# A three-layer cross network with a ReLU tower: layer 2 fed before layer 1 is normalized, one norm matmul for three layers, other orders of the first loads and of the top layers

## The chip, the cores and the metric

The kernel runs on one core of one Trainium2 chip. The metric is the device time of one launch in microseconds (us); lower is better. Three timed runs of the kernel before gave 1300.02, 1300.39 and 1301.56 us, median 1300.39.

## The reference

Everything is fp32. For each of 512 samples, 39 table rows of 16 numbers are gathered (`e`, 512 x 39 x 16). Three cross layers follow, each with 128 units; `ws[k]` and `bs[k]` are their weights and biases:

```python
prev = x                                   # b, 39, 16
for k in range(3):
    z = jnp.einsum('bmd,bhd->bdmh', x, prev).reshape(b, D, m * h)
    t = jnp.einsum('bdc,co->bdo', z, ws[k]) + bs[k]
    t = jnp.transpose(t, (0, 2, 1))
    norm = jnp.sqrt(jnp.sum(t * t, axis=(-2, -1), keepdims=True))
    t = t / norm
    logit.append(t)
    prev = t
z = jnp.sum(jnp.concatenate(logit, axis=1), axis=-1)          # b, 384
h = jnp.concatenate([z, dense_ctx], axis=1)                   # b, 400
h = jnp.maximum(h @ W_top1 + b_top1, 0.0)                     # 512
h = jnp.maximum(h @ W_top2 + b_top2, 0.0)                     # 256
y = h @ W_top3
```

The norm is one number for each sample, over all 128 units and 16 positions. Below the layers are called layer 0, 1 and 2.

## The kernel before, in words

The batch is cut into 16 tiles of 32 samples. In a tile, the free axis of every operand has 512 columns (32 samples times 16 positions, `N`), and the partitions hold fields or units.

**Gather.** GpSimd computes row numbers and issues ten indirect DMAs a tile into `gathered` (L154), waits for them, writes the rows to DRAM (`xt`, L162 and L164), waits for that and goes on to the next tile. It runs far ahead: every tile has its own place in `xt`.

**Loads.** SyncE's queue (SP) brings the tile's rows back. `load_layer0` (L184 to L190) issues eight DMAs: three copies of the 39 fields into `x3` and the shifted fields into `xr`. `load_fields` (L199) issues thirteen DMAs of 768 KB into `xb`, in which each field is repeated over all 128 partitions; chunk c holds three fields. For every tile but the first, chunk c is loaded when layer 2 of the tile before has used it. The weights of layers 1 and 2 (`w1`, `w2`, 2.5 MB each) are issued at the very start from ScalarE's queue (L224, L225).

**Layer 0.** VectorE multiplies `x3` by each of the seven steps of `xr` into `z0` (`products0`, L295) and TensorE accumulates seven matmuls into `acc[0]` (L392). It is symmetric, so seven steps of three shifts do.

**Layers 1 and 2.** VectorE multiplies three fields at a time, 128 x 1536 numbers, by the layer before (`t_ps[0]` or `t_ps[1]`, in PSUM) into one of four slots of `z` (`products`, L308; thirteen chunks a layer), and TensorE runs three matmuls on each chunk (`layer`, L405). An fp32 matmul shows as two instructions in the trace, so a layer is 78 of them.

**Normalizing.** After each layer, ScalarE squares the accumulator and adds the bias (L243, L245), VectorE sums both over positions (`sum_squares`, L316 and L318), TensorE adds over partitions with a matmul with ones on 32 columns (`add_partitions`, L414), ScalarE takes the root (L250), and VectorE refines the inverse (`normalize`, L328 to L335), writes the normalized layer to `t_ps[k]` (L339, layers 0 and 1) and the sums to `feat` (L344). All three layers have a chain of their own.

**Order.** Each engine's program is written out by hand. In tile i, TensorE runs layer 1 of i, layer 0 of i+1, layer 2 of i. VectorE runs the products of layer 1 (with the sums and the normalizing of layer 2 of tile i-1 put between chunks), `products0(i + 1)`, then the whole normalizing of layer 1 of tile i, and then the products of layer 2 (with the normalizing of layer 0 of tile i+1 between chunks).

**Top.** After the last tile, the weights of the tower lie in the space of `xb` (loaded after the last product), and TensorE runs 16 matmuls for the first dense layer (L453, L454; three accumulators, the fourth output block waits for one), 8 for the second (L459) and 2 for the output (L464).

Of the kernel before, what the change touches and what calls it, by code (L numbers as in the profile page):

```python
# [35 lines left out]


CH = 3
CHUNKS = FIELDS // CH
ZSLOTS = 4  # L40

TOP1, TOP2 = 512, 256
DENSE = 16


def build(nc, ids_in, base_in, table, xt, dense_t, w0a, w0b, w1, w2, b0, b1, b2,
          wt1, bt1, wt2, bt2, wt3, out):
    ctx = ExitStack()
    with ctx:
# [15 lines left out]
        z0 = sb("z0", [WIDE, STEPS0, N])  # L65
# [6 lines left out]
        ones = sb("ones", [P, P])  # L72
        traw = sb("traw", [P, LAYERS, N])
# [8 lines left out]
        feat = sb("feat", [P, LAYERS, BATCH])  # L82
        dense_sb = sb("dense_sb", [DENSE, BATCH])
        bt1_sb = sb("bt1_sb", [P, TOP1 // P])
        bt2_sb = sb("bt2_sb", [P, TOP2 // P])
        wt3_sb = sb("wt3_sb", [P, TOP2 // P])

        top = xb[:, :, :].rearrange("p m n -> p (m n)")
        wt1_sb = top[:, 0:LAYERS * TOP1].rearrange("p (k o) -> p k o", k=LAYERS)
        wt1d_sb = top[0:DENSE, LAYERS * TOP1:4 * TOP1]  # L90
        wt2_sb = top[:, 4 * TOP1:4 * TOP1 + 4 * TOP2].rearrange("p (k o) -> p k o", k=4)
# [6 lines left out]
        nrm = [pb(f"nrm{k}") for k in range(LAYERS)]  # L98
# [6 lines left out]
        w_loaded = [None, sem("w1_loaded"), sem("w2_loaded")]  # L105
        small_loaded = sem("small_loaded")
        w0_ready = sem("w0_ready")
        ones_ready = sem("ones_ready")
        x0_loaded = sem("x0_loaded")
# [4 lines left out]
        acc0_ready = sem("acc0_ready")  # L114
        raw_ready = [sem(f"raw_ready{k}") for k in range(LAYERS)]
        ssum_ready = [sem(f"ssum_ready{k}") for k in range(LAYERS)]
        nrm_ready = [sem(f"nrm_ready{k}") for k in range(LAYERS)]
        root_ready = [sem(f"root_ready{k}") for k in range(LAYERS)]
        step_done = sem("step_done")
        rnorm_ready = [sem(f"rnorm_ready{k}") for k in range(LAYERS)]  # L120
        t_ready = [sem("t0_ready"), sem("t1_ready")]
        feat_ready = [sem(f"feat_ready{k}") for k in range(LAYERS)]
        top_loaded = sem("top_loaded")
# [3 lines left out]


        ZSTEPS = 2 * CHUNKS

        def slot_free(i, s):

            if s >= ZSLOTS:
                return ZSTEPS * i + s - ZSLOTS + 1
            last = max(r for r in range(ZSTEPS) if r % ZSLOTS == s)
            return None if isinstance(i, int) and i == 0 else ZSTEPS * (i - 1) + last + 1
# [4 lines left out]
        def _(pool):  # L141
            nc.gpsimd.memset(ones[:, :], 1.0).then_inc(ones_ready, 1)
            pool.wait_ge(ids_loaded, 32)

            def gather(i):


# [9 lines left out]
                pool.wait_ge(rows_gathered, 16 * GROUPS * (i + 1))  # L157

                for first, rows in ((0, FIELDS), (FIELDS, SHIFTS - 1)):
                    full, rest = divmod(rows, GROUP)  # L160
                    blk = xt[bass.ds(i, 1), first:first + rows, :].rearrange("a m n -> (a m) n")
                    pool.dma_start(blk[0:full * GROUP, :].rearrange("(g f) (b d) -> (f b) g d", f=GROUP, d=EMB),  # L162
                                   gathered[:, 0:full, :]).then_inc(xt_written, 16)
                    pool.dma_start(blk[full * GROUP:rows, :].rearrange("f (b d) -> (f b) d", d=EMB),  # L164
                                   gathered[0:rest * TILE_B, full, :]).then_inc(xt_written, 16)

                pool.wait_ge(xt_written, 64 * (i + 1))

            with pool.Fori(0, TILES) as i:
                gather(i)  # L170

        @block.sync
        def _(sp):
# [5 lines left out]
            def load_layer0(i):  # L179

# [11 lines left out]
            def load_fields(i):  # L192
                later = not (isinstance(i, int) and i == 0)
                for c in range(CHUNKS):
                    if later:

                        sp.wait_ge(z_ready, ZSTEPS * (i - 1) + CHUNKS + c + 1)
# [85 lines left out]
        def _(dve):  # L283
# [14 lines left out]
            def products(i, k, c):  # L298

                s = (k - 1) * CHUNKS + c  # L300
                if c == 0:
                    dve.wait_ge(t_ready[k - 1], i + 1)
# [210 lines left out]
```

## Time and profile before

| | |
|---|---|
| median of three timed runs | 1300.39 us |
| span of the profiled execution | 1297.4 us |
| TensorE matmul busy | 1217.8 us, 94% |
| VectorE busy | 904.4 us, 70% |
| ScalarE busy | 78.1 us, 6% |
| GpSimd busy | 205.2 us, 16% |
| DMA | 203.70 MB, mean 157 GB/s |

The profiled execution has its span alone as its time, from the first instruction to the last; the timed runs are 3.0 us longer at the median, which lies around the span. In the rows below, "PE" is TensorE's matmuls, "DVE" VectorE, "ACT" ScalarE, "SPq" the DMA issues of SyncE. A row of the chain says when a piece began, how long it was on the chain and what it was; x78 counts instructions. A row of the windows shows a stretch, the busy time of each engine in it, then the granted TensorE clock as a share of full speed, the mean busy share of the 16 DMA engines, and GB/s.

### The profile page before, as it was taken

How to read it: one execution, taken by the hardware profiler on the slowest of the kernel's cores; microseconds unless marked ns; L12 is line 12 of the kernel's file. 1: busy time of each engine (PE TensorE's matmuls, PEld its weight loads, DVE VectorE, ACT ScalarE, POOL GpSimd, SP SyncE). 2: the span in 40 equal slices, each digit the busy share in tenths (PEclk: the TensorE clock that was granted, in tenths of full speed). 3: DMA queues.
4: the chain of work that ended last, by engine and by line, in shares of the span. 5: the costliest groups of instructions: out<-in, count | busy, mean ns of one | idle time of the engine just before them, and what ended most of it. 6: DMA issues, size and time to landing. Idle time of an engine off the chain costs nothing.

```text
span 1297.4 us, 9951 instructions
## 1 busy us (share of the span) xinstructions
PE 1217.8 (94%) x2868; PEld 538.6 (42%) x2868; DVE 904.4 (70%) x898; ACT 78.1 (6%) x155; POOL 205.2 (16%) x245
## 2 busy tenths in 40 slices
PE   0599999999999999999999999999999999999898
PEld 0244444444444444444444444444444444444343
DVE  0468877777787777778777777887777788777640
ACT  0100000000000000000000000000000000000001
POOL 5554654546440000000000000000000000000000
PEclk9899999999999999999999999999999999999998
DMA  7938356290935528092653809165380917444010
GB/s 221 361 58 314 75 195 194 70 316 12 325 63 202 170 87 285 0 323 49 219 153 107 265 0 332 39 233 138 121 250 9 330 32 254 118 145 170 1 41 0
DMA packets 58974, 203.70 MB, mean 157 GB/s; under 512 B 11131, under 2 KB 14331, under 8 KB 58966
## 3 DMA queue, kind: packets, MB, share of 16 engines
q1 hardware_dynamic: 47478, 195.26, 46.1%
q0 software_dynamic: 7424, 3.19, 1.8%
q10 hardware_dynamic: 4064, 5.15, 1.2%
q8 instruction: 4, 0.07, 0.0%
q14 instruction: 4, 0.03, 0.0%
HBM read 201.67 MB, written 1.90 MB: 157 GB/s over the span
## 4 chain that ended last, share of the span: by engine, by line
PE 91%; DVE 4%; issue 2%; DMA 2%; ACT 1%; POOL 1%; SPq 0%; POOLq 0%; ACTq 0%
PE acc L405 83%; PE acc L392 5%; DVE z L308 2%; PE acc L453 1%; DMA xr<-xt 1%; PE nrm L414 1%; POOL gathered L154 1%; PE t_ps L459 1%; DVE inv L328 1%; DMA gathered<-in_table,rows_of 0%; PE acc L454 0%; ACT root L250 0%; DVE prod L330 0%; DVE rnorm L335 0%; DVE half L332 0%
## 5 line engine op out<-in xcount | busy, mean ns | idle before, releaser
L405 PE MATMUL acc<-z,w_sb 128*128 128x512 f32 x2496 | 1087.4, 596 | 27.4 <-DVE z L308 27.4
L308 DVE TENSOR_TENSOR z<-t_ps,xb 128x1536 f32<-128x1536 f32 x416 | 711.9, 1751 | 186.0 <-PE acc L405 185.6
L405 PEld LDWEIGHTS acc<-z,w_sb 128*128 128x128 f32 x2496 | 472.4, 191 | 617.7 <-issue 545.8
L154 POOL DMA_INDIRECT gathered<-in_table,rows_of x160 | 154.3, 964 | 57.6 <-issue 43.9
L392 PE MATMUL acc<-z,w_sb 117*128 117x512 f32 (+1 forms) x224 | 104.4, 609 | 40.7 <-DVE z L295 40.7
L316 DVE TENSOR_REDUCE ssum<-sq 128x32 f32<-128x512 f32 x48 | 32.6, 679 | 111.6 <-ACT traw L245 111.6
L295 DVE TENSOR_TENSOR z<-x,xr 117x512 f32<-117x512 f32 (+1 forms) x112 | 68.8, 682 | 29.5 <-DMA xr<-xt 29.5
L243 ACT ACTIVATE sq<-acc,bias 128x512 f32<-128x512 f32 x48 | 33.0, 687 | 808.8 <-PE acc L405 771.8
L392 PEld LDWEIGHTS acc<-z,w_sb 117*128 117x128 f32 (+1 forms) x224 | 42.1, 194 | 88.1 <-issue 87.1
L162 POOL DMA_DIRECT2D xt<-gathered x32 | 29.8, 932 | 76.9 <-DMA gathered<-in_table,rows_of 74.4
L245 ACT ACTIVATE traw<-acc,bias 128x512 f32<-128x512 f32 x48 | 32.7, 681 | 0.0
L318 DVE TENSOR_REDUCE dsum<-traw 128x32 f32<-128x512 f32 x48 | 32.4, 675 | 0.0
L414 PEld LDWEIGHTS nrm<-ssum,ones 128*128 128x128 f32 x96 | 18.2, 193 | 31.6 <-issue 21.5
L328 DVE RECIPROCAL inv<-root 128x32 f32<-128x32 f32 x48 | 16.6, 345 | 19.1 <-ACT root L250 18.8
L250 ACT ACTIVATE root<-nrm 128x32 f32<-128x32 f32 x48 | 9.5, 198 | 335.9 <-PE nrm L414 335.8
L339 DVE TENSOR_TENSOR t_ps<-traw,rnorm 128x512 f32<-128x512 f32 x32 | 22.4, 699 | 1.1
L414 PE MATMUL nrm<-ssum,ones 128*128 128x32 f32 x96 | 15.2, 240 | 7.6 <-DVE ssum L316 7.6
L164 POOL DMA_DIRECT2D xt<-gathered x32 | 18.1, 564 | 0.0
L453 PE MATMUL acc<-feat,xb 128*128 128x512 f32 x24 | 14.0, 728 | 1.7 <-DVE feat L344 1.7
L148 POOL TENSOR_TENSOR rows_of<-ids_sb,base_sb 128x10 int32<-128x10 int32 x16 | 3.1, 196 | 48.3 <-DMA xt<-gathered 45.3
L344 DVE TENSOR_TENSOR feat<-dsum,rnorm 128x32 f32 (+1 forms) x48 | 8.9, 186 | 2.3 <-DVE rnorm L335 2.2
L335 DVE SCALAR_TENSOR_TENSOR rnorm<-half,inv 128x32 f32<-128x32 f32 x48 | 9.2, 191 | 1.6
(23 smaller groups left out, 51.1 us busy)
## 6 DMA issues: line engine op xcount, KB each, us to landing
xb<-xt SPq DMA_DIRECT2D x208, 768.0 KB, 6.4
xr<-xt SPq DMA_DIRECT2D x48, 468.0 KB
x<-xt SPq DMA_DIRECT2D x48, 78.0 KB
gathered<-in_table,rows_of POOLq DMA_INDIRECT x160
xr<-xt SPq DMA_DIRECT2D x32, 78.0 KB
xt<-gathered POOLq DMA_DIRECT2D x16, 72.0 KB, 2.9
xb<-in_wt SPq DMA_DIRECT2D x1, 768.0 KB, 4.6
xt<-gathered POOLq DMA_DIRECT2D x32, 6.0 KB, 2.1
```

The costliest lines, as they stand in the source:

```text
L154: nc.gpsimd.indirect_dma_start(gathered[0:n, g, :], None, table[:, :], bass.IndirectOffsetOnAxis(rows_of[0:n, g:g + 1], 0)).then_inc(rows_ ...
L162: pool.dma_start(blk[0:full * GROUP, :].rearrange("(g f) (b d) -> (f b) g d", f=GROUP, d=EMB), gathered[:, 0:full, :]).then_inc(xt_written ...
L243: nc.scalar.activation(sq[:, k, :], acc[k][:, :], ACT.Square, bias=bias[:, k:k + 1]).then_inc(raw_ready[k], 1)
L245: nc.scalar.activation(traw[:, k, :], acc[k][:, :], ACT.Identity, bias=bias[:, k:k + 1]).then_inc(raw_ready[k], 1)
L295: nc.vector.tensor_tensor(z0[0:n, k, :], x3[0:n, :], xr[0:n, k, :], ALU.mult).then_inc(z0_ready, 1)
L308: nc.vector.tensor_tensor(z[:, s % ZSLOTS, :, :], fields_of(k, c), xb[:, c * CH:(c + 1) * CH, :], ALU.mult).then_inc(z_ready, 1)
L316: nc.vector.tensor_reduce(ssum[:, k, :], sq[:, k, :].rearrange("p (b d) -> p b d", d=EMB), axis=AX_X, op=ALU.add).then_inc(ssum_ready[k], 1)
L318: nc.vector.tensor_reduce(dsum[:, k, :], traw[:, k, :].rearrange("p (b d) -> p b d", d=EMB), axis=AX_X, op=ALU.add).then_inc(step_done, 1)
L328: nc.vector.reciprocal(inv[:, k, :], root[:, k, :]).then_inc(step_done, 1)
L392: last = nc.tensor.matmul(acc[0][:, :], w0_sb[0:n, k, :], z0[0:n, k, :], start=(k == 0), stop=(k == STEPS0 - 1))
L405: last = nc.tensor.matmul(acc[k][:, :], w_sb[k][:, m, :], z[:, s % ZSLOTS, r, :], start=(m == 0), stop=(m == FIELDS - 1))
L414: nc.tensor.matmul(nrm[k][:, 0:TILE_B], ones[:, :], ssum[:, k, :], start=True, stop=True).then_inc(nrm_ready[k], 1)
```

## The change

Four things are changed together.

1. **Layer 2 gets layer 1 with its bias but without its norm.** ScalarE writes `acc[1]` plus bias straight to `t_ps[1]`; `products(i, 2, c)` waits for that alone. As layer 2 is linear in layer 1 up to its bias, the accumulator of layer 2 is multiplied by layer 1's inverse norm afterwards, once, by VectorE (`scale2`, in the next tile's layer 1 after chunk 2), into `scaled`, from which ScalarE makes the squares and the biased copy.
2. **One norm event a tile.** The sums of layer 2 of tile i-1, layer 1 of tile i and layer 0 of tile i+1 lie side by side in `ssum`; one matmul of 96 columns (`add_partitions`, after chunk 4 of layer 2), one root and one `normalize` (after chunk 6) serve them all. `feat` is written for three layers at once.
3. **First loads and queues.** GpSimd only gathers; the writes to `xt` and the wait for them stand in SyncE's queue (`write_rows`). `products0` writes its result over `xr`, so that the loads of tile i+1 wait for `acc0_ready` of tile i, and `xr` is loaded in four groups with a semaphore each. For the first tile ScalarE's queue loads `x3`. `w1` is cut into thirteen pieces, issued by SyncE between the pieces of `xb`, and `w2` behind them. ScalarE runs a Sqrt on one column at the start.
4. **Top.** The tower's weights have space of their own and are loaded during tile 0. The matmuls that need only layers 0 and 1 and the dense inputs (now padded to 128 partitions) come first, the last norm matmul stands between them, and the four that need layer 2 come last. Four accumulators; the second dense layer loops over its inputs outside.

The core of the diff:

```diff
@@ ScalarE
+            act.wait_ge(ones_ready, 1)
+            nc.scalar.activation(warm[:, :], ones[:, 0:1], ACT.Sqrt)
...
+            act.wait_ge(xt_written, 64)
+            for j in range(PER_STEP):
+                act.dma_start(x3[j * FIELDS:(j + 1) * FIELDS, :],
+                              xt[0, 0:FIELDS, :]).then_inc(x3_loaded, 16)
...
+            def evacuate1(i):
+                act.wait_ge(z_used, ZSTEPS * i + CHUNKS)
+                nc.scalar.activation(t_ps[1][:, :], acc[1][:, :], ACT.Identity,
+                                     bias=bias[:, 1:2]).then_inc(t1_ready, 1)
+                if not (isinstance(i, int) and i == 0):
+                    act.wait_ge(feat_ready, i + 1)
+                add_bias(1, acc[1][:, :])
...
             def tile(i, first=False, last=False):
                 if not first:
-                    evacuate(2, i - 1)
-                    square_root(2, i - 1)
-                evacuate(1, i)
-                square_root(1, i)
+                    evacuate2(i - 1)
+                evacuate1(i)
                 if not last:
-                    evacuate(0, i + 1)
-                    square_root(0, i + 1)
+                    evacuate0(i + 1)
+                square_root(i + 1, *layers_of(first, last))
@@ VectorE
             def tile(i, first=False, last=False):
                 for c in range(CHUNKS):
                     products(i, 1, c)
-                    if c == 3 and not first:
-                        sum_squares(2, i - 1)
-                    if c == 6 and not first:
-                        normalize(2, i - 1, 3 * i)
+                    if c == 2 and not first:
+                        scale2(i - 1)
+                    if c == 5 and not first:
+                        sums(2, i - 1)
                 if not last:
                     products0(i + 1)
-                sum_squares(1, i)
-                normalize(1, i, 3 * i + 1)
                 for c in range(CHUNKS):
                     products(i, 2, c)
+                    if c == 2:
+                        sums(1, i)
                     if c == 3 and not last:
-                        sum_squares(0, i + 1)
-                    if c == 6 and not last:
-                        normalize(0, i + 1, 3 * i + 2)
+                        sums(0, i + 1)
+                    if c == 6:
+                        normalize(i + 1, *layers_of(first, last))
+                        if not last:
+                            scale0(i + 1)
@@ TensorE
             def tile(i, first=False, last=False):
-                layer(i, 1, range(0, 4))
-                if not first:
-                    add_partitions(2, i - 1)
-                layer(i, 1, range(4, CHUNKS))
+                layer(i, 1, range(CHUNKS), first)
                 if not last:
-                    layer0(i + 1, range(0, 4))
-                add_partitions(1, i)
-                if not last:
-                    layer0(i + 1, range(4, STEPS0))
-                layer(i, 2, range(0, 4))
-                if not last:
-                    add_partitions(0, i + 1)
-                layer(i, 2, range(4, CHUNKS))
+                    layer0(i + 1)
+                layer(i, 2, range(0, 5), first)
+                add_partitions(i + 1, *layers_of(first, last))
+                layer(i, 2, range(5, CHUNKS), first)
...
             for j in range(TOP1 // P):
-                if j == 3:
-                    pe.wait_ge(h1_ready, 1)
                 o = slice(j * P, (j + 1) * P)
-                for k in range(LAYERS):
-                    nc.tensor.matmul(acc[j % 3][:, :], wt1_sb[:, k, o], feat[:, k, :], start=(k == 0), stop=False)
...
+                if j == 2:
+                    add_partitions(TILES + 1, 2, 3)
+                for k in range(LAYERS - 1):
+                    nc.tensor.matmul(h1_ps[j][:, :], wt1_sb[:, k, o], feat[:, k, :], start=(k == 0), stop=False)
+                nc.tensor.matmul(h1_ps[j][:, :], wt1d_sb[:, o], dense_sb[:, :], start=False, stop=False)
+            pe.wait_ge(feat_ready, TILES + 2)
+            for j in range(TOP1 // P):
+                o = slice(j * P, (j + 1) * P)
+                nc.tensor.matmul(h1_ps[j][:, :], wt1_sb[:, LAYERS - 1, o], feat[:, LAYERS - 1, :],
                                  start=False, stop=True).then_inc(h1_acc, 1)
@@ SyncE
+            write_rows(0)
+            load_layer0(0, with_x3=False)
+            w1_rows = w1.rearrange("(m h) o -> h m o", h=P)
+            for c in range(CHUNKS):
+                load_field_chunk(0, c)
+                sp.dma_start(w_sb[1][:, c * CH:(c + 1) * CH, :],
+                             w1_rows[:, c * CH:(c + 1) * CH, :]).then_inc(w1_loaded[c], 16)
+            sp.dma_start(w_sb[2][:, :, :], w2.rearrange("(m h) o -> h m o", h=P)).then_inc(w2_loaded, 16)
+            write_rows(1)
+            sp.wait_ge(acc0_ready, 1)
+            load_layer0(1)
+            sp.dma_start(wt1_sb[:, :, :], wt1[0:LAYERS * P, :].rearrange("(k p) o -> p k o", p=P)
+                         ).then_inc(small_loaded, 16)
...
             with sp.Fori(1, TILES - 1) as i:
                 load_fields(i)
-
+                write_rows(i + 1)
+                sp.wait_ge(acc0_ready, i + 1)
                 load_layer0(i + 1)
             load_fields(TILES - 1)
```

## Rows read from the trace of the kernel before

**Rows 1.** The chain of waits, one steady tile: start us, us, what.

```profile
694.94 3.44 PE acc L392 x8
...
700.67 1.77 DVE z L308
...
702.49 10.57 PE acc L405 x24
713.05 0.14 PE nrm L414 x2
713.19 33.56 PE acc L405 x78
...
770.15 3.43 PE acc L392 x8
...
777.69 10.57 PE acc L405 x24
```

**Rows 2.** The chain of waits, the last tile and the top layers.

```profile
1221.42 0.69 ACT sq L243
...
1227.84 36.27 PE acc L405 x78
...
1268.25 5.46 PE acc L453 x6
...
1286.36 7.06 PE t_ps L459 x16
1293.42 1.82 PE nrm L464 x4
```

**Rows 3.** The chain of waits, from the start to layer 2 of tile 0.

```profile
16.68 5.16 DMA gathered<-in_table,rows_of
...
24.98 1.66 DMA xt<-gathered
...
29.59 10.28 DMA xr<-xt
...
40.73 8.45 PE acc L392 x14
...
49.25 1.28 ACT L243
...
51.23 0.59 ACT traw L245
...
57.18 36.20 PE acc L405 x78
...
100.84 0.70 PE acc L405
```

**Rows 4.** The timeline of VectorE in a steady tile: normalizing layer 0.

```profile
713.52 0.34 DVE L328 RECIPROCAL inv<-root 128x32 f32<-128x32 f32 x1
...
715.28 5.08 DVE L308 TENSOR_TENSOR z<-t_ps,xb 128x1536 f32<-128x1536 f32 x3
```

**Rows 5.** The windows: five engines, granted clock, DMA share, GB/s.

```profile
10.00:12.00 2.00, 0.00 (x0) 0.00 (x0) 0.41 (x2) 0.00 (x0) 1.39 (x3) 1.00 1.06 375
...
40.00:45.00 5.00, 4.27 (x5) 1.83 (x6) 4.19 (x7) 0.00 (x0) 0.51 (x1) 1.00 1.03 405
...
50.00:55.00 5.00, 0.64 (x2) 0.50 (x2) 2.66 (x7) 3.28 (x5) 0.36 (x2) 0.70 1.03 407
...
65.00:70.00 5.00, 5.00 (x13) 2.18 (x12) 3.52 (x2) 0.00 (x0) 1.87 (x2) 1.00 0.87 176
```

**Rows 6.** The timeline of SyncE: first issue of layer 0's loads, tile 1 and steady.

```profile
53.38 0.33 SPq L184 DMA_DIRECT2D x<-xt  x1
...
728.74 0.33 SPq L184 DMA_DIRECT2D x<-xt  x1
```

**Rows 7.** The windows behind those loads in a steady tile, and in the last tile.

```profile
740.00:745.00 5.00, 5.00 (x13) 2.22 (x12) 5.00 (x5) 0.00 (x0) 0.00 (x0) 1.00 0.43 83
...
1225.00:1227.00 2.00, 0.00 (x0) 0.00 (x0) 1.97 (x4) 0.00 (x0) 0.00 (x0) 0.79 0.01 4
```

More of the change, by code:

```diff
@@ L134, in slot_free, with layers_of @@
                 return ZSTEPS * i + s - ZSLOTS + 1
-            last = max(r for r in range(ZSTEPS) if r % ZSLOTS == s)
-            return None if isinstance(i, int) and i == 0 else ZSTEPS * (i - 1) + last + 1
+            before = max(r for r in range(ZSTEPS) if r % ZSLOTS == s)
+            return None if isinstance(i, int) and i == 0 else ZSTEPS * (i - 1) + before + 1
+        def layers_of(first=False, last=False):
+            return (1 if last else 0), (2 if first else 3)
         block = ctx.enter_context(nc.Block())
@@ L156, in gather @@
                         bass.IndirectOffsetOnAxis(rows_of[0:n, g:g + 1], 0)).then_inc(rows_gathered, 16)
[L157 to L169, printed above, removed]
+            gather(0)
+            with pool.Fori(1, TILES) as i:
                 gather(i)
@@ L177, in _, with write_rows @@
             sp.dma_start(w0_sb[:, :, :], w0a).then_inc(w0a_loaded, 16)
-            def load_layer0(i):
+            def write_rows(i):
+                sp.wait_ge(rows_gathered, 16 * GROUPS * (i + 1))
+                for first, rows in ((0, FIELDS), (FIELDS, SHIFTS - 1)):
+                    full, rest = divmod(rows, GROUP)
+                    blk = xt[bass.ds(i, 1), first:first + rows, :].rearrange("a m n -> (a m) n")
+                    sp.dma_start(blk[0:full * GROUP, :].rearrange("(g f) (b d) -> (f b) g d", f=GROUP, d=EMB),
+                                 gathered[:, 0:full, :]).then_inc(xt_written, 16)
+                    sp.dma_start(blk[full * GROUP:rows, :].rearrange("f (b d) -> (f b) d", d=EMB),
+                                 gathered[0:rest * TILE_B, full, :]).then_inc(xt_written, 16)
@@ L380, in _, with layer0, layer @@
             tile(TILES - 1, last=True)
[L381 to L382 removed]
+            scale2(TILES - 1)
+            sums(2, TILES - 1)
+            normalize(TILES + 1, 2, 3)
         @block.tensor
         def _(pe):
[L386 to L389 removed]
+            def layer0(i):
+                if not (isinstance(i, int) and i == 0):
+                    pe.wait_ge(raw_ready[0], i)
+                for k in range(STEPS0):
                     n = WIDE if k < STEPS0 - 1 else NARROW
                     pe.wait_ge(z0_ready, STEPS0 * i + k + 1)
[L392 removed]
+                    last = nc.tensor.matmul(acc[0][:, :], w0_sb[0:n, k, :], xr[0:n, k, :],
                                             start=(k == 0), stop=(k == STEPS0 - 1))
[L394 to L397 removed]
+                last.then_inc(acc0_ready, 1)
+            def layer(i, k, chunks, first=False):
                 for c in chunks:
                     if c == 0 and not (isinstance(i, int) and i == 0):
[L400 removed]
+                        pe.wait_ge(raw_ready[1] if k == 1 else scaled_ready, i)
+                    if k == 1 and first:
+                        pe.wait_ge(w1_loaded[c], 16)
+                    if k == 2 and first and c == 0:
+                        pe.wait_ge(w2_loaded, 16)
                     s = (k - 1) * CHUNKS + c
```

277 lines of the change are left out of this document (143 added, 134 removed).

## The prediction

> **What bounds the kernel now.** I read three views: the chain of waits over one steady tile, the same chain at both ends, and the windows for clock and DMA.
>
> In the steady tile the reader should see that TensorE's work sets the time [rows 1]. Layer 2 starts at 702.49 in one tile and 777.69 in the next: 75.20 us. A layer's 78 instructions take 33.56, 0.4303 each; two layers are 67.12 and layer 0's 14 are 6.02. Three norm matmuls cost 0.14 each. That makes 73.56. The other 1.64 is between layers 0 and 2: layer 0 starts at 694.94 and would end at 701.1 (6.02 and a norm matmul), but layer 2 starts at 702.49, because the chunk that it needs was only begun at 700.67, after the norm chain of layer 1. The first 24 instructions of layer 2 then take 10.57 where 24 x 0.4303 is 10.33. So 1.4 of waiting and 0.24 of restart.
>
> At the ends [rows 2, 3]: layer 2 of tile 0 starts at 100.84; layer 1 of tile 15 ends at 1221.40, layer 2 starts 6.44 later and takes 36.27, since the clock fell; from its end at 1264.11 the tower runs to 1295.24, and 2.16 remain to the end of the span.
>
> **Steady tiles.** Layer 2's first chunk now waits for one ScalarE pass (0.69) [rows 2] after layer 1's end, 770.15 in the row. By 771.1 `t_ps[1]` is there; VectorE, which has finished `products0` before, needs 1.77: 772.9, and TensorE ends layer 0 at 776.2. The wait is gone with 3.3 to spare. The three norm matmuls become one of 96 columns. No row shows that width: it costs at least the 0.14 of 32 columns and at most three times that; most of 0.14 is there whatever the columns, so I take 0.20. A tile is then 67.12 + 6.02 + 0.20 = 73.34, which saves 1.86. Bounds: 73.28 to 73.56.
>
> What is late next is `normalize` after chunk 6 of layer 2. TensorE reaches the norm matmul after five chunks, 12.9 after the layer's start, where it was after four. VectorE can begin chunk 6 when chunk 2 has freed its slot (3 x 2.58 = 7.74), has it ready at 9.6 and then waits; root and inverse begin at 13.6; from inverse to next product took 715.28 - 713.52 = 1.76 [rows 4]. With 64 more elements in five instructions, at the slope between a 32 element one (0.19) and a 512 element one (0.70), that is 0.07 each, 0.33 in all; the inverse may scale with all its excess and add 0.3. Chunk 7 is made from 15.7 (or 16.0) to 17.4 (17.7), and TensorE needs it at 12.9 + 0.2 + 2 x 2.58 = 18.3. Cover 0.6 to 0.9: I cost it at nothing. If the chain is longer than that, each us costs 15. `scale2` (0.70, as the pass to `t_ps` it replaces) stands behind chunk 2 of layer 1; chunk 3 then is ready 1.7 before TensorE asks. Sums of layers 0 and 1 end 4.4 after layer 2's start, far before 12.9.
>
> ScalarE has one more pass of 0.69 for layer 1 and two roots fewer; it idles most of a tile.
>
> **SP's queue in steady tiles.** `write_rows(i+1)` now stands before layer 0's loads. Those were issued from 728.74, 26.25 after layer 2's start [rows 6], and the last data came by about 742 (83 GB/s over 740 to 745) [rows 7]. Now four writes come first and land behind the last `xb` pieces, 6 to 8 us, and six more issues cost 2: done about 50 after layer 2's start. Layer 0 begins 67.3 after it. Hidden, with over 15 to spare. The wait for `acc0_ready` is long met, so `products0` in place costs nothing in steady tiles.
>
> **The start.** Rows landed in `gathered` at 21.84, the writes at 26.64 after four GpSimd issues [rows 3]. SP issues about 0.4 each: I take 25.5, 1.1 earlier (bounds 24.8 and 27.5, since no row shows these small writes from SP). The loads of layer 0 took until 39.87, all awaited together. They run slowly (176 GB/s in 65 to 70, when they have the queue) [rows 5]. The first group with `x3` is 0.7 MB, so VectorE starts about 31 instead of 39.89; the last group lands about 38.5, and layer 0 ends about 40.5 where it ended at 49.18. If TensorE stays at half clock through such a broken stream, add 3.
>
> From there to layer 1 took 8.0 (57.18 - 49.18). The table load of 1.28 at 49.25 goes, as the early Sqrt loads it, and VectorE's first sum no longer waits for the biased copy (0.59). Layer 1 starts 6.2 after layer 0: 46.7, and with the same cold stretch takes 36.20: until 82.9.
>
> But the weights moved. Between 10 and 22 us the DMA engines ran at 375 GB/s on `w1` and `w2` [rows 5], under the gather, at no cost. Now those 5.1 MB stand in SP's queue with 10.2 MB of `xb`, and **behind them `write_rows(1)`, then layer 0's loads of tile 1**. From 38.5: a pair of pieces is 0.79 MB at 405 GB/s and 0.20 MB at 375 [rows 5], 2.5 in all; the thirteenth lands at 70.7 and is needed at 78.5 (the chunk's 1.8 and its matmuls' 2.6 before 82.9), so layer 1 doesn't wait. `w2` takes 6.8 more: 77.5. The writes land at 79, SP wakes, and the 1.84 MB of tile 1 need from then about 11.5 (1.3 to the first byte, 10.2 at about 180 GB/s): last group 90.5. VectorE's last step of layer 0 ends 91.2, its chunk for layer 2 is behind it in order, 93.0. Layer 2 of tile 0 starts at **93.0** instead of 100.84: the 10.5 won before layer 1 shrink to 7.8. If nothing stood behind the weights, 82.9 + 6.02 = 88.9; if the queue drains at 350 GB/s all through, 98.
>
> The row that speaks for this order is tile 1's loads before: issued from 53.38 behind `xb` [rows 6], they moved at their own slow rate only after 64.
>
> The Trainium skill ("DMA: Bandwidth & Descriptors", Queues, rings and completion order) says that one engine's rings are drained in order and that the DMA engines alternate between the queue rows of different issuers. That is a rule against this change: GpSimd's writes could slip between SP's pieces, SP's own can't. By it layer 2 starts near 93, without it at 88.9; the rows give the same.
>
> **Tile 15 and the top.** After 14 periods: 93.0 + 14 x 73.34 + 67.3 (layer 2 of tile 14, layer 1 of tile 15) = 1187.1. No layer 0 hides the step: ScalarE 0.69, chunk 1.77 and hand-overs make 2.56 instead of 6.44. The clock was seen to fall 2.8 us after work stopped at 49.18 (0.70 in 50 to 55, so at 52.0) [rows 5] and 4.8 after 1221.4 (0.79) [rows 7]; a stop of 2.56 is shorter, so I take full clock: 33.56 + 0.24 + 0.20 = 34.0, until 1223.7. If it falls, 2.7 more.
>
> The tower: 12 matmuls that wait for nothing new (10.3) cover the chain of layer 2 (scale 0.70, square 0.69, sum 0.70, norm matmul at 5.2, root and `normalize` done by 7.2), then 4: 16 x 0.861 + 0.14 = 13.9. Then 7.06 and 1.82 [rows 2]: 22.8 where it was 31.13, of which 2.8 is a cold stretch (5.46 for six instructions). Ends at 1246.5, span 1248.7.
>
> **Sum.** 7.8 + 14 x 1.86 (26.0) + 0.4 + 3.9 (gap) + 2.3 (clock) + 8.3 (top) = 48.7. The span before is 1297.4, the median 3.0 above it; I keep that 3.0: 1300.39 - 48.7 = **1251.6**.
>
> **Rivals.**
> - *Late `normalize`.* The chain from norm matmul to chunk 7 takes 1.4 more than I think, 0.7 beyond the cover: 15 x 0.7 = 10.5, 1262. For it: VectorE idles in front of it in every tile. Against: each piece has a row.
> - *Free queue in tile 0.* The writes overtake or the drain is quicker: layer 2 at 88.9, 1247.5. Against: [rows 6].
> - *The wait stays.* Something holds the first chunk of layer 2, and steady tiles save only the 0.24 of norm matmuls: 1251.6 + 14 x 1.6 = 1274. Against: 3.3 of slack.
> - *Slower: SP's queue late in every tile.* If writing and reading the rows back ends later than 71 after layer 2's start (forecast 50), each us more costs 14. It decides at 21 + 48.7/14 = 24.5 us later; at 27 later 14 x 6 = 84, 1336. For it: write, wait and read are now serial in a queue that already holds 10 MB. Against: DMA stands still after 743 in the steady tile.
>
> **How the numbers follow.** Forecast 0.67 (its own range 1247 to 1257: queue in tile 0, the clock in tile 15), late `normalize` 0.13, free queue 0.12, wait stays 0.05, SP late 0.03. The range leaves out the last two and the far end of the second: 1245 to 1263. A measurement tells about 0.2% from no change. Faster: all but the last case and a rest for causes not seen, 0.95; same 0.01; slower 0.04.
>
> **What would show it.** In the profile after: layer 2 starts 73.3 apart, no idle of TensorE between layers 0 and 2; one norm matmul a tile; VectorE idle before the inverse and chunk 7 just in time; in tile 0 VectorE waiting for `xr` behind layer 1, layer 2 near 93; a gap near 2.6 in tile 15, at full clock; the top in 22.8. The prediction is wrong if a bubble stands at chunk 7, or tile 0's loads miss by more than 5.

## The result

The changed kernel took 1245.01 us (median of four, 1242.94 to 1247.43) against 1300.2 us for the kernel before on the same chip: ratio 0.9572, interval 0.9553 to 0.9592. The forecast was 1251.6 with a range of 1245 to 1263. The way and most of the size were right; the result lies at the lower edge of the range (0.9572 of 1300.39 is 1244.7, just under it), 6.6 us faster than said. The span of the profiled execution fell from 1297.4 to 1240.9.

The page of the changed kernel, part 1:

```profile
PE 1201.1 (97%) x2808; PEld 531.4 (43%) x2808; DVE 877.9 (71%) x748; ACT 81.6 (7%) x139; POOL 157.5 (13%) x183
```

The chain of waits of the changed kernel in a steady tile; L448 is layer 0, L464 layers 1 and 2, L474 the norm matmul:

```profile
667.22 6.01 PE acc L448 x14
673.24 12.88 PE acc L464 x30
686.11 0.19 PE nrm_ps L474 x2
686.31 54.10 PE acc L464 x126
```

Nothing but TensorE stands on it: layer 0 ends and layer 2 begins in the same instant, where [rows 1] had 1.4 us and VectorE's chunk between them. The norm matmul of 96 columns takes 0.19 in its row. From one layer 0 to the next are 73.19 us.

VectorE in the same tile, from the timeline of the changed kernel:

```profile
681.00 1.76 DVE L353 TENSOR_TENSOR z<-t_ps,xb 128x1536 f32<-128x1536 f32 x1 [0.50 <-PE acc L464]
...
686.62 0.75 DVE L378 RECIPROCAL inv<-root 128x96 f32<-128x96 f32 x1 [3.87 <-ACT root L292]
...
689.18 10.07 DVE L353 TENSOR_TENSOR z<-t_ps,xb 128x1536 f32<-128x1536 f32 x6
```

Chunk 6 is ready at 682.8, VectorE waits 3.87 for the root, and from inverse to next product it takes 2.56, where three times narrower it was 1.76 [rows 4]. Chunk 7 is ready at 690.9; TensorE asks at 686.31 + 2 x 2.58 = 691.5.

The start, from the chain of the changed kernel (SPq is SyncE's issue):

```profile
16.08 2.38 DMA gathered<-in_table,rows_of
...
20.06 1.55 DMA xt<-gathered
...
56.52 11.61 SPq L188
...
70.40 2.12 DMA xt<-gathered
...
77.11 6.67 DMA xr<-xt
83.80 0.70 DVE xr L339
...
84.55 2.84 PE acc L448 x6
...
87.51 13.11 PE acc L464 x30
```

And TensorE's timeline there:

```profile
28.01 9.33 PE L448 MATMUL acc<-xr,w_sb 117*128 117x512 f32 x14 [28.01 <-issue]
...
43.32 35.97 PE L464 MATMUL acc<-z,w_sb 128*128 128x512 f32 x78 [4.07 <-DVE z L353]
...
79.35 1.95 PE L448 MATMUL acc<-xr,w_sb 117*128 117x512 f32 x4
```

The reader should set this beside [rows 3]. The first tile's rows are gathered at 18.46 (21.84 before), written at 21.61 (26.64), layer 1 starts at 43.32 (57.18). Then the queue that the prediction feared shows: the first write of tile 1's rows (L188) is held 11.61 us at its issue behind `xb` and the weights, the writes land at 72.5, layer 0's loads at 83.8, and TensorE stops twice in layer 0 before layer 2 starts at 87.51 (100.84 before).

The end, from the chain of the changed kernel (L280 writes `t_ps[1]`; L505 is the tower's first matmul, L515 its second layer):

```profile
1179.57 0.67 ACT t_ps L280
...
1182.17 13.11 PE acc L464 x30
...
1195.45 20.66 PE acc L464 x48
1216.10 1.72 PE acc L505 x4
...
1221.25 0.14 PE nrm_ps L474 x2
1221.39 1.80 PE h1a_ps L505 x4
...
1230.06 6.87 PE t_ps L515 x16
1236.92 1.82 PE nrm_ps L521 x4
```

Against [rows 2]: the stop between layers 1 and 2 of tile 15 is 2.63 instead of 6.44, layer 2 takes 33.94 instead of 36.27, and the tower follows without a gap, 22.65 instead of 31.13.

So the 56.5 us of span: 13.3 by layer 2 of tile 0, 28.0 in fourteen periods (14 x 2.01, less 0.2 for the restart behind tile 0's stop), 0.5 in the two layers after them, 3.8 and 2.3 in tile 15, 8.5 in the tower.

### The profile page after: what moved, and what is told of

Same layout as the page of the kernel before. It is cut to its first block, busy times and chain, and to the rows that moved or that the text cites. A ratio compares the mean times of both kernels' runs of the same rounds, so it can differ in the third digit from the quotient of the medians.

```text
span 1240.9 us, 9676 instructions
## 1 busy us (share of the span) xinstructions
PE 1201.1 (97%) x2808; PEld 531.4 (43%) x2808; DVE 877.9 (71%) x748; ACT 81.6 (7%) x139; POOL 157.5 (13%) x183
## 4 chain that ended last, share of the span: by engine, by line
PE 93%; SPq 4%; DMA 1%; POOL 1%; issue 1%; DVE 0%; ACT 0%; POOLq 0%
PE acc L464 84%; PE acc L448 7%; SPq L218 1%; SPq L188 1%; SPq L210 1%; POOL gathered L167 1%; PE t_ps L515 1%; SPq L203 1%; DMA xr<-xt 1%; DMA xt<-gathered 0%; PE acc L505 0%; PE nrm_ps L474 0%; DMA gathered<-in_table,rows_of 0%; SPq L190 0%; DMA base_sb<-in_base 0%
## 5 line engine op out<-in xcount | busy, mean ns | idle before, releaser
L464 PE MATMUL acc<-z,w_sb 128*128 128x512 f32 x2496 | 1079.6, 593 | 6.8 <-DVE z L353 6.7
L464 PEld LDWEIGHTS acc<-z,w_sb 128*128 128x128 f32 x2496 | 473.5, 190 | 597.9 <-issue 571.4
L448 PE MATMUL acc<-xr,w_sb 117*128 117x512 f32 (+1 forms) x224 | 102.6, 609 | 29.3 <-issue 28.6
L339 DVE TENSOR_TENSOR xr<-x,xr 117x512 f32<-117x512 f32 (+1 forms) x112 | 69.0, 686 | 31.4 <-DMA x<-xt 18.3
L448 PEld LDWEIGHTS acc<-xr,w_sb 117*128 117x128 f32 (+1 forms) x224 | 43.3, 195 | 85.4 <-issue 82.9
L378 DVE RECIPROCAL inv<-root 128x96 f32<-128x96 f32 (+2 forms) x18 | 12.4, 687 | 60.9 <-ACT root L292 60.8
L280 ACT ACTIVATE t_ps<-acc,bias 128x512 f32<-128x512 f32 x16 | 10.6, 662 | 461.1 <-PE acc L464 421.2
L268 ACT ACTIVATE sq<-scaled,bias 128x512 f32<-128x512 f32 x16 | 11.6, 722 | 387.8 <-issue 268.8
L268 ACT ACTIVATE sq<-acc,bias 128x512 f32<-128x512 f32 x32 | 21.9, 683 | 98.4 <-PE acc L448 92.1
L269 ACT ACTIVATE traw<-acc,bias 128x512 f32<-128x512 f32 x32 | 21.9, 684 | 0.0
L362 DVE TENSOR_TENSOR scaled<-acc,rnorm 128x512 f32<-128x512 f32 x16 | 10.9, 682 | 8.5 <-PE acc L464 8.5
L269 ACT ACTIVATE traw<-scaled,bias 128x512 f32<-128x512 f32 x16 | 11.3, 707 | 0.0
L474 PEld LDWEIGHTS nrm_ps<-ssum,ones 128*128 128x128 f32 x36 | 6.8, 190 | 10.5 <-issue 8.1
L396 DVE TENSOR_TENSOR t_ps<-traw,rnorm 128x512 f32<-128x512 f32 x16 | 11.1, 694 | 0.0
L474 PE MATMUL nrm_ps<-ssum,ones 128*128 128x96 f32 (+2 forms) x36 | 6.4, 259 | 1.5 <-DVE ssum L369 1.5
L515 PE MATMUL t_ps<-z,wt_sb 128*128 128x512 f32 x16 | 7.0, 592 | 0.0
```

The lines of the kernel that those rows point to most:

```text
L268: nc.scalar.activation(sq[:, k, :], src, ACT.Square, bias=bias[:, k:k + 1]).then_inc(sq_ready[k], 1)
L269: nc.scalar.activation(traw[:, k, :], src, ACT.Identity, bias=bias[:, k:k + 1]).then_inc(raw_ready[k], 1)
L339: nc.vector.tensor_tensor(xr[0:n, k, :], x3[0:n, :], xr[0:n, k, :], ALU.mult).then_inc(z0_ready, 1)
L448: last = nc.tensor.matmul(acc[0][:, :], w0_sb[0:n, k, :], xr[0:n, k, :], start=(k == 0), stop=(k == STEPS0 - 1))
L464: last = nc.tensor.matmul(acc[k][:, :], w_sb[k][:, m, :], z[:, s % ZSLOTS, r, :], start=(m == 0), stop=(m == FIELDS - 1))
L474: nc.tensor.matmul(nrm_ps[:, k0 * TILE_B:k1 * TILE_B], ones[:, :], ssum[:, k0:k1, :].rearrange("p k b -> p (k b)"), start=True, stop=True) ...
```

## The experiments

Twelve kernels ran, four to a chip, each timed against the kernel before on its chip; the control ran on the first chip only, so from `e4_top_in_order` on a difference to it is one of two ratios from two chips. Numbers in brackets behind a ratio are its interval; where a few us are at stake the rows of the profiles decide, since the intervals are 2.4 us wide to either side.

**The changed kernel again** (`c1_control`).

> The changed kernel again, as the one to compare with on this chip. It should give 0.957 of the kernel before, and the profile again: first gather landed near 18.5, layer 2 of tile 0 at 87.5, tiles 73.2 apart.

Ratio 0.9567 [0.9548, 0.9586], 1244.52 us, span 1240.7; layer 2 of tile 0 at 87.22. Its chain at the start:

```profile
16.02 2.17 DMA gathered<-in_table,rows_of
```

**Both weights at the start** (`e1_weights_at_start`).

```diff
@@ ScalarE, behind the loads of bias
+            act.dma_start(w_sb[1][:, :, :], w1.rearrange("(m h) o -> h m o", h=P)).then_inc(w1_loaded[0], 16)
+            act.dma_start(w_sb[2][:, :, :], w2.rearrange("(m h) o -> h m o", h=P)).then_inc(w2_loaded, 16)
...
@@ SyncE
             for c in range(CHUNKS):
                 load_field_chunk(0, c)
-                sp.dma_start(w_sb[1][:, c * CH:(c + 1) * CH, :],
-                             w1_rows[:, c * CH:(c + 1) * CH, :]).then_inc(w1_loaded[c], 16)
-            sp.dma_start(w_sb[2][:, :, :], w2.rearrange("(m h) o -> h m o", h=P)).then_inc(w2_loaded, 16)
...
```

> w1 and w2 are issued whole from ScalarE's queue at the start, as in the kernel before; all else is the changed kernel. Theory (the weights' 5.1 MB slowed the first gather before, and that is the term I left out): the first tile's rows land in gathered at 21.8 instead of 18.5, layer 1 of tile 0 starts near 46.7 instead of 43.3; SP's queue is 14 us of data lighter, so tile 1's loads are hidden and layer 2 of tile 0 starts at 46.7 + 36.0 + 6.0 = 88.7, 1.2 later: about 1.2 us slower than the control. Rival (the gather is quicker for another reason, such as who issues the writes): it still lands at 18.5, layer 1 starts at 43.3, layer 2 at 85.3, 2.2 us faster than the control.

Ratio 0.9567 [0.9548, 0.9586], 1244.65 us: even. Its chain:

```profile
16.34 5.15 DMA gathered<-in_table,rows_of
...
23.09 1.54 DMA xt<-gathered
...
45.92 35.51 PE acc L463 x78
81.43 6.01 PE acc L447 x14
87.44 12.88 PE acc L463 x30
```

The last gather DMA needs 5.15 us from its issue with the weights beside it and 2.17 without, all else equal: the weights cost the gather 3.0 us. And without them SP's queue is in time: layer 0 of tile 1 is one block of 6.01. Layer 1 of tile 0 starts at 45.92 (43.25 in the control, 46.7 expected), layer 2 at 87.44 (87.22, 88.7 expected). Moving the weights behind the gather gave 2.7 us at layer 1 and took 2.5 back by layer 2. The theory holds for the gather, and the start as a whole came 0.8 to 1.3 us earlier than it said; the rival (the gather at 18.5) fell.

**w2 last** (`e2_w2_last`).

```diff
@@ SyncE, after the thirteen pairs
-            sp.dma_start(w_sb[2][:, :, :], w2.rearrange("(m h) o -> h m o", h=P)).then_inc(w2_loaded, 16)
             write_rows(1)
             sp.wait_ge(acc0_ready, 1)
             load_layer0(1)
+            sp.dma_start(w_sb[2][:, :, :], w2.rearrange("(m h) o -> h m o", h=P)).then_inc(w2_loaded, 16)
```

> w2 (2.6 MB) is issued behind tile 1's row writes and layer 0 loads instead of ahead of them. Theory (SP's queue holds up tile 0's step to layer 2): the writes of tile 1 land 6 to 7 us earlier, near 66, its loads end near 77, TensorE goes from layer 1 to layer 0 to layer 2 without a stop, layer 2 starts at 79.3 + 6.0 = 85.3 instead of 87.5: 2.2 us faster, unless w2, issued near 72, lands after 85 with 1.9 MB ahead of it (then up to 2 slower). Rival (TensorE or VectorE set that step, not the loads): no change.

Ratio 0.955 [0.953, 0.9569], 1243.25 us; by the ratios alone not clear of the control. In the profile layer 0 of tile 1 is one block (80.75, 6.01) and layer 2 follows at 86.76. This execution began a little late (the first write is issued at 19.50, in the control at 18.20); from that issue to layer 2 of tile 0 are 67.3 us, 69.0 in the control: 1.8 us gained, 2.2 expected. The size is rough: the eight profiles with the changed kernel's start have 68.2 to 70.0 there. `w2` came in time.

**w1 at the start** (`e3_w1_at_start`): the first added line of `e1_weights_at_start` and the removal of the thirteen pieces of `w1`; `w2` stays in SP's queue.

> w1 alone is issued at the start from ScalarE's queue (2.6 MB, done near 11 us, before the last gather is issued), w2 stays in SP's queue ahead of tile 1's rows. Theory: the first gather still lands at 18.5, as only the last of its ten DMAs is waited for; layer 1 starts at 43.3; SP's queue is 7 us lighter, tile 1's loads are hidden and layer 2 of tile 0 starts at 85.3: 2.2 us faster than the control. Rival (any load beside the gather delays it by its share): landing near 20.1, layer 2 near 87, about even.

Ratio 0.9545 [0.9527, 0.9564], 1242.53 us; by the ratios not clear of the control either. The chain, at the gather, at tile 0 and at layer 2 of tile 15, and a window there:

```profile
16.78 2.32 DMA gathered<-in_table,rows_of
...
80.26 6.01 PE acc L447 x14
86.28 12.88 PE acc L463 x30
...
1180.70 14.81 PE acc L463 x30
```

```profile
1182.00:1186.00 4.00, 4.00 (x7) 1.63 (x6) 4.00 (x5) 0.00 (x0) 0.00 (x0) 0.57 0.01 4
```

The last gather DMA takes 2.32 us with `w1` alone at the start, as without any weights (2.17 to 2.38): the theory holds, the rival fell. From the first write (19.12) to layer 2 are 67.2: 1.9 gained, 2.2 expected. The later rows show something else: thirty instructions that took 13.11 in the changed kernel's profile take 14.81 here, at a granted clock of 0.57 just after the same stop of 2.6 us. The profiles of `e1_weights_at_start`, `e2_w2_last` and `e5_three_norms` have the same 14.81. The changed kernel's own profile was one of the executions without it. The mean granted clocks of its four timed runs point the same way: 0.997, 0.995, 0.997 and 0.995, at spans of 1240.9, 1244.4, 1241.4 and 1245.4.

**The top in its old order** (`e4_top_in_order`).

```diff
             pe.wait_ge(small_loaded, 7 * 16)
-            pe.wait_ge(feat_ready, TILES + 1)
             pe.wait_ge(raw_ready[1], TILES)
+            add_partitions(TILES + 1, 2, 3)
+            pe.wait_ge(feat_ready, TILES + 2)
             for j in range(TOP1 // P):
...
-                if j == 2:
-                    add_partitions(TILES + 1, 2, 3)
-                for k in range(LAYERS - 1):
+                for k in range(LAYERS):
...
-            pe.wait_ge(feat_ready, TILES + 2)
...
```

> Only the order of the first dense layer's matmuls is undone: the norm matmul of layer 2 comes first, TensorE waits for all three features, then runs the 16 matmuls block by block. Theory (the top's gain is the chain of layer 2 covered by 12 matmuls, plus the clock kept): TensorE idles about 5.1 us after its last chunk (scale 0.7, square 0.7, sum 0.7, norm matmul 0.4, root 0.25, inverse and refinement 1.5, hand-overs), the clock falls and the first matmuls lose 2.8: 8 us slower than the control, near 1252.5. Rival (the clock is no part of it): 5 slower.

Ratio 0.9636 [0.9618, 0.9654], 1252.71 us, 0.0069 or 9.0 us slower than the control; 8 was expected. Its chain, and two windows:

```profile
1218.74 0.70 DVE scaled L362
...
1223.12 4.54 PE acc L504 x6
...
1238.82 6.87 PE t_ps L510 x16
```

```profile
1222.00:1224.00 2.00, 0.88 (x2) 0.50 (x3) 0.93 (x5) 0.00 (x0) 0.00 (x0) 0.95 0.00 0
1224.00:1226.00 2.00, 2.00 (x3) 0.66 (x2) 0.00 (x0) 0.00 (x0) 0.00 (x0) 0.50 0.00 0
```

TensorE stops 4.4 us (1218.72 to 1223.12, one norm matmul in it), and the first six instructions take 4.54 instead of 2.58: 1.96 more, of which 0.24 is the restart seen behind every stop and 1.7 is clock. So the rows give the order 6.2: 4.26 of stop (the norm matmul of 0.14 is in both) and 1.96. The span is 9.0 longer than the control's, but 1.45 of it is again the step at tile 15, 14.56 where the control has 13.11, and 1.4 stands ahead of it: layer 1 of tile 15 ends at 1180.73, in the control at 1179.29. The 9.0 of the ratios is uncertain by more than 3 either way, so it doesn't contradict 6.2. The expectation was near by its number only: both its terms were too large, 5.1 of stop (4.3 measured) and 2.8 of clock (1.7). The rival, that the clock has no part, is refuted by the second window. The clock fell after work had begun again: full until about 1223.8, half from there.

**Three norm matmuls for one** (`e5_three_norms`).

```diff
-                nc.tensor.matmul(nrm_ps[:, k0 * TILE_B:k1 * TILE_B], ones[:, :],
-                                 ssum[:, k0:k1, :].rearrange("p k b -> p (k b)"),
-                                 start=True, stop=True).then_inc(nrm_ready, 1)
+                for k in range(k0, k1):
+                    last = nc.tensor.matmul(nrm_ps[:, k * TILE_B:(k + 1) * TILE_B], ones[:, :], ssum[:, k, :],
+                                            start=True, stop=True)
+                last.then_inc(nrm_ready, 1)
```

> The one norm matmul of 96 columns is made three of 32 columns, at the same place and with one event as before. Theory (a norm matmul costs mostly a fixed 0.14, so that three for one is the 0.2 to 0.25 I took): each tile 0.23 longer, 3.5 us slower in all, near 1248. Rival (the columns cost as much as the instruction): no change.

Ratio 0.963 [0.9613, 0.9647], 1252.14 us: 0.0063 or 8.2 us slower, not 3.5. Its chain:

```profile
689.04 0.59 PE nrm_ps L475 x6
689.62 54.16 PE acc L464 x126
```

Three together stand in the chain with 0.59, and the wide instructions behind them take 0.08 more than 126 times 0.4292. The period is 73.63 instead of 73.19 us, 0.44 longer. That is 6.5 us up to the end of layer 1 of tile 15 and 0.2 in tile 15; 1.7 more is the clock there, absent in the control's profile. Both theories missed the price. The row of a norm matmul alone misleads, as it leaves out that the wide instruction behind it takes longer: in the tower of the changed kernel, four instructions behind the norm matmul take 1.80 instead of 1.72. Row and delay together, by the starts in the traces, a norm matmul of 32 columns costs 0.22 (0.14 and 0.08), one of 64 costs 0.22 (0.17 and 0.06) and one of 96 costs 0.22 (0.19 and 0.03). Three of 32 columns in a row cost 0.67, three times the same. So they cost no more side by side than apart, and making one of three saves 0.45 a tile. Why each costs that much wasn't tried.

**The norm matmul one chunk later** (`e6_norm_later`) **and one earlier** (`e6b_norm_earlier`).

```diff
-                layer(i, 2, range(0, 5), first)
+                layer(i, 2, range(0, 6), first)
                 add_partitions(i + 1, *layers_of(first, last))
-                layer(i, 2, range(5, CHUNKS), first)
+                layer(i, 2, range(6, CHUNKS), first)
```

> The norm matmul stands one chunk later in TensorE's order (after six chunks of layer 2 instead of five), VectorE's order as it is. Theory (the cover of normalize is 0.4 us in this kernel's profile, 690.9 against 691.3): chunk 7 is then ready 2.2 us after TensorE asks for it, a stop in each of 16 tiles, 35 us slower, near 1280. Rival (there is more slack than the profile shows, as slots of z buffer it): under 5 slower.

> The norm matmul stands one chunk earlier (after four chunks). The sums it needs end about 4 us after layer 2 starts, 6 us before. Theory (normalize is fully covered already): no change, within 0.5 us. Rival (the late chain costs something in every tile that the rows don't show): faster by 15 times that.

Later: ratio 0.9901 [0.9882, 0.9919], 1287.04 us, 43 us slower than the control. Its chain and two windows:

```profile
710.47 0.21 PE nrm_ps L474 x2
...
713.55 1.76 DVE z L353
...
715.35 20.01 PE acc L464 x46
```

```profile
638.00:640.00 2.00, 1.88 (x4) 0.90 (x5) 2.00 (x3) 0.00 (x0) 0.00 (x0) 0.81 0.40 123
640.00:642.00 2.00, 2.00 (x3) 0.78 (x3) 2.00 (x2) 0.00 (x0) 0.00 (x0) 0.50 1.00 396
```

TensorE finishes chunk 6 at 713.27 and chunk 7 starts at 715.35: a stop of 2.1, and with the restart the period grows from 73.19 to 75.53, by 2.34. Fifteen of them are 35.1, and tile 15 stops some 1.3 longer: about 36.4, near the 35 expected. The rest of the 43.1 by which the span is longer is clock: behind three of the fifteen stops, four tiles apart, it falls (the windows show the one at 638), and 114 instructions take 50.89 where 49.19 is usual; the stop of 2.6 before layer 2 of tile 15 is followed by a fall as well, and 36 instructions take 17.39 instead of 15.69. Four times 1.70 is 6.8, 43.2 together. Earlier: ratio 0.9562 [0.9545, 0.958], 1243.72 us, no change; here the clock held at tile 15 (24 instructions behind the stop in 10.54). So `normalize` is covered in the changed kernel, by 0.5 us and no more.

**The feed of layer 2 last** (`e7_feed_last`).

```diff
             def evacuate1(i):
                 act.wait_ge(z_used, ZSTEPS * i + CHUNKS)
-                nc.scalar.activation(t_ps[1][:, :], acc[1][:, :], ACT.Identity,
-                                     bias=bias[:, 1:2]).then_inc(t1_ready, 1)
                 if not (isinstance(i, int) and i == 0):
                     act.wait_ge(feat_ready, i + 1)
                 add_bias(1, acc[1][:, :])
+                nc.scalar.activation(t_ps[1][:, :], acc[1][:, :], ACT.Identity,
+                                     bias=bias[:, 1:2]).then_inc(t1_ready, 1)
```

> ScalarE writes the unnormalized layer 1 to t_ps[1] after the square and the biased copy instead of ahead of them, 1.27 us later in every tile. Theory (the old wait is gone with 3.4 us to spare in steady tiles: the first chunk of layer 2 is ready at 669.8 in the profile, TensorE asks at 673.2): the period stays 73.19; in tile 0 the loads set the step anyway; only tile 15, where nothing hides it, stops 1.3 longer, and the clock falls there for certain: 1.3 to 3 us slower than the control. Rival (the slack is smaller than it looks): 15 times what is missing, up to 19 slower.

Ratio 0.9589 [0.9571, 0.9607], 1247.76 us, 2.9 us slower by the ratios, whose intervals don't quite separate it from the control. Its chain in tile 15:

```profile
1182.72 0.56 ACT t_ps L283
...
1185.21 15.86 PE acc L464 x30
```

Steady tiles are unchanged (layer 2 of tile 8 starts 585.7 after that of tile 0, 8 x 73.2); in tile 15 the stop is 3.8, and thirty instructions take 15.86, 2.75 more than at full clock. This profile is of the slowest of the four runs (granted clock 0.993; two others have 0.996), so the clock fell less in these, and that it falls in tile 15 each time isn't shown; 2.2 of the 6.0 us by which its span is longer stand ahead of layer 2 of tile 0. The old wait is gone with room, as the prediction had it.

**The steady part alone** (`e8_steady_part_alone`): the changed kernel with GpSimd's writes, loads and waits of layer 0, weights at the start and no early Sqrt, as in the kernel before, and with the top of `e4_top_in_order`.

```diff
-LOADS0 = [(0, 2), (2, 4), (4, 6), (6, 7)]
+LOADS0 = [(0, 6), (6, 7)]
...
-            nc.scalar.activation(warm[:, :], ones[:, 0:1], ACT.Sqrt)
...
@@ GpSimd, gather(i)
-                if not (isinstance(i, int) and i == 0):
-                    pool.wait_ge(xt_written, 64 * i)
...
+                pool.wait_ge(rows_gathered, 16 * GROUPS * (i + 1))
+                for first, rows in ((0, FIELDS), (FIELDS, SHIFTS - 1)):
...
+                pool.wait_ge(xt_written, 64 * (i + 1))
```

> The steady part of the change alone: layer 2 fed unnormalized, one norm event, products over xr. The start is undone (GpSimd writes the rows, both weights from ScalarE's queue at the start, all loads of layer 0 awaited together, no early Sqrt), and so is the order of the top's first layer. Theory: 14 periods shorter by 2.01 (28.2), tile 15's stop shorter by 3.8, 1.4 at tile 0's step, 1 to 2.5 of clock, 0.6 in the first norm chain, 2.3 from the tower's four accumulators and padded inputs: 38 us, near 1262. Rival (the period gained from the loads' new place): periods near 74, 1272.

Ratio 0.97 [0.9684, 0.9717], 1261.43 us: 39.0 us (0.030 of 1300) faster than the kernel before, 38 expected. Layer 2 in its timeline, two tiles running:

```profile
684.86 13.04 PE L455 MATMUL acc<-z,w_sb 128*128 128x512 f32 x30
...
758.05 2.31 PE L455 MATMUL acc<-z,w_sb 128*128 128x512 f32 x5
```

73.19 apart, as in the whole change: the loads' new place has no part in the period. Start and top are then worth 17.3 us together (0.0133), and 18.9 by the spans of the profiles: 12.1 of start (layer 1 of tile 15 ends at 1191.33, in the control at 1179.26) and 6.9 of tower (29.52 from layer 2's end where the control has 22.64), of which `e4_top_in_order` has 6.2. The tower's 8.5 against the kernel before hold 6.2 of order by the rows; the rest, 1.6 to 2.3 (29.52 here, 28.79 in `e4_top_in_order`, 31.13 before), is left for the fourth accumulator and the padded inputs, which weren't tried apart. Nor does a run put the old feed of layer 2 back into the changed kernel: that its wait made the 1.6 us of stop and restart in a steady tile is read from the two chains, while the 0.45 of the norm matmuls is measured by `e5_three_norms`.

**Filling the stop** (`e10_fill_alone`), **and a version meant to be faster** (`e9_best`), which has besides `w1` at the start and the norm matmul after four chunks.

```diff
@@ TensorE, tile
                 if not last:
                     layer0(i + 1)
+                else:
+                    pe.wait_ge(small_loaded, 7 * 16)
+                    pe.wait_ge(feat_ready, TILES)
+                    for j in (2, 3):
+                        o = slice(j * P, (j + 1) * P)
+                        nc.tensor.matmul(h1_ps[j][:, :], wt1_sb[:, 0, o], feat[:, 0, :], start=True, stop=False)
+                        nc.tensor.matmul(h1_ps[j][:, :], wt1d_sb[:, o], dense_sb[:, :], start=False, stop=False)
...
```

> The changed kernel with only those four matmuls moved into tile 15's stop. Theory (the stop of 2.6 us, which the profile of the change passed at full clock, lets the clock fall in most executions): 2.6 us for the stop minus 0.8 by which the filling is longer, plus the 0.8 returned in the top, plus on average about 1.2 of clock: 3.5 us faster than the control, near 1241, and layer 2 of tile 15 takes 33.7 to 34.0 always. Rival (the clock held in most executions): 2.6 faster.

> A version meant to be faster: w1 at the start from ScalarE's queue (2 us by the run with that alone), the norm matmul after four chunks, and four of the tower's first matmuls (layer 0's features and the dense inputs, for two output blocks) run in tile 15 between layers 1 and 2, where TensorE stopped for 2.6. Theory: 1.9 from w1, 2.6 for the stop, which is filled by work taken out of the top, and 0.8 to 1.7 as the clock can't fall there: about 1239, with a narrower spread. Rival (moving the matmuls opens a wait in the top, where only eight then cover the chain of layer 2): 1241.

Filling alone: ratio 0.9553 [0.9536, 0.957], 1241.68 us, 1.8 us faster than the control by the ratios, which their intervals don't separate; spans of the profiles 1238.4 and 1240.7, and the thirty instructions of layer 2 take 12.88. From the end of layer 1 of tile 15 to the tower's end are 56.34 us where the control has 59.20: 2.9 gained, the stop of 2.6 and the restart; its start was 0.6 later. That is the rival's 2.6; the further 1.2 of clock that the theory added on average doesn't show in the median. Its four runs are as far apart (1240.55 to 1243.57) as the control's, so the stop in tile 15 is not all of the spread. The faster version: ratio 0.9522 [0.9508, 0.9535], 1238.14 us (1236.99 to 1238.61), 4.8% faster than the kernel before and 5.9 us faster than the changed one; 1239 was expected. Its chain:

```profile
1176.65 0.86 PE h1a_ps L486 x2
...
1180.08 10.30 PE acc L463 x24
...
1213.78 0.86 PE acc L509 x2
```

TensorE has no stop from 43.35 to the tower's last matmuls.

## Why the prediction was near, and where it failed

**The failed term is tile 0's start.** The prediction said that the weights were loaded "under the gather, at no cost", and carried the landing of the rows, 21.84, into the changed kernel. It moved the weights and kept the delay that they had caused. Without them the gather lands at 18.46, and `e1_weights_at_start` shows that it is they: 5.15 us from the last issue to landing with them, 2.17 without. The Trainium skill ("DMA: Bandwidth & Descriptors", Issuing engines are not separate DMA queues) has the DMAs of all issuers run on the same 16 DMA engines and interleave. The trace agrees, with the 5.15 us against 2.17. I applied that rule to what the weights would delay in their new place and not to what they had delayed in the old one.

The other parts of that path were each a little shorter than said: the writes 3.15 instead of 3.66, tile 0's loads of layer 0 about 11.5 instead of 13, the drain to tile 1's writes about 39 instead of 40.5; only the last step was longer, 3.7 instead of 2.5, because the last two groups landed together and three steps and a chunk stood behind them. Layer 2 of tile 0 came at 87.51 instead of 93.0: 5.5 of the 6.6 us, and the landing of the gather is 3.4 of these.

**The queue that was feared is real, and small.** Tile 1's rows stood behind the weights as said; it cost 2.2 us against 85.3 (79.3 + 6.0). `e2_w2_last` and `e3_w1_at_start` got 1.8 and 1.9 of it back in two ways.

**Steady tiles.** 73.34 was said, 73.19 measured, 1.9 us over fourteen periods. The term for the norm matmuls was mis-sized: 0.14 each and 0.20 for the wide one, a saving of 0.22, where three cost 3 x 0.22 and one costs 0.22, a saving of 0.45. The missing 0.08 behind each was in the prediction's 0.4303 for a wide instruction and in its 1.64 of stop: by their starts the wide instructions follow each other at 0.4292 in both kernels. With that, the period before is 170 x 0.4292 + 0.67 + 1.57 of stop and restart, and the new one 72.96 + 0.22. The cover of `normalize` was given as 0.6 to 0.9 and is 0.5: the inverse took 0.75 at 96 elements, 0.35 at 32, so it grows with all its excess. `e6_norm_later` shows what it is worth.

**Tile 15.** Stop 2.56 said, 2.63 measured; 34.0 said, 33.94 measured. But the argument for the full clock, that 2.6 is shorter than the shortest stop with a fall that I had seen, is wrong: of the ten profiles with this stop six lose 1.45 to 1.7 behind it, and `e6_norm_later` loses 1.70 behind three of its fifteen stops of 2.1. That the profile of the changed kernel passed it at full clock was luck; the median may carry part of that cost.

**The top.** 22.8 said, 22.65 measured; `e4_top_in_order` gives 6.2 by its rows, 9.0 by the ratios, for the order alone. Here the prediction's mechanism and size are both borne out.

**Around the span.** I kept 3.0 us between span and time. A timed run of the kernel before is mostly 1.6 to 2.0 above its own span, at most 2.8 (a run of 1298.70 has a span of 1297.0), so its profiled execution was one of the quicker. The changed kernel's median is 4.1 above its profiled span, that of the quickest of its four runs. This gave back 1.1 of the 7.8 by which the span was wrong.

The rivals: late `normalize`, the wait that stays and SP's queue late in every tile did not occur. The free queue in tile 0 was wrong as a mechanism, the queue being there, but its time, 1247.5, is nearer than the forecast.

## What to carry to other kernels

When a load is moved, price both places: what it will delay where it goes, and what it was delaying where it stood; a duration read beside other traffic isn't the duration without it. A stop of TensorE of two to three us may cost its clock as well, mostly after the work has begun again, in some executions and not in others; filled with matmuls that are due later anyway, this one cost neither in the two profiles that have it so. The row of a short instruction can leave out part of its price; compare the period with it and without. A norm chain placed by hand has a cover that can be read off as the distance between a chunk's end and its matmul: 0.5 us here, and one place later in the order cost 43 us.

## What the hardware showed that I had not expected

- The clock can fall after a stop of 2.1 us, and the fall can come once work is running again: in `e6_norm_later` three of fifteen such stops lose 1.70 each; behind 2.6 us in tile 15 thirty instructions took 13.11 in three profiles (two of the changed kernel, one of the steady part alone) and 14.56 or 14.81 in five. With the norm matmul moved, `e6b_norm_earlier` held the clock there and `e6_norm_later` lost 1.70.
- A norm matmul costs TensorE 0.22 us at 32, at 64 and at 96 columns, apart or three in a row; its row in the chain shows only 0.14 to 0.20 of that.
- VectorE's reciprocal takes 0.35, 0.55 and 0.75 us for 32, 64 and 96 elements a partition, 6.3 ns an element, where the other small operations go from 0.19 to 0.26.
